# Spreading delta first and du three units ahead, with replanned slots and all low parts as transfers, in a Mamba and MoE layer

## The chip, the cores and the metric

One core of one Trainium2 chip. The metric is the device time of one execution in microseconds (us); the lower, the better. TensorE is called PE here, VectorE DVE, ScalarE ACT, GpSimd POOL and SyncE SP.

## What is computed

The reference is a layer on 32 x 256 tokens of width 128: `x + attn(layernorm(x)) + ffn(layernorm(x))`. `attn` is a Mamba block (inner width 256, 4 heads of 64 channels, 16 states) and `ffn` a mixture of 8 experts with top-1 routing and a capacity of 1024 tokens each.

```python
xz = hidden_states @ in_proj_w.T                    # x, z
x = silu(conv4(x) + conv_b)
dt_r, Bm, Cm = split(x_proj(x))
delta = softplus(dt_proj(dt_r) + dt_proj_b)
def step(s, inp):                                   # over the 256 steps of a sequence
    d_t, u_t, B_t, C_t = inp
    dA = jnp.exp(d_t[..., None] * A)
    s = s * dA + (d_t * u_t)[..., None] * B_t[:, :, None, :]
    y_t = jnp.einsum('bhdn,bhn->bhd', s, C_t)
y = (y + x * Dskip) * silu(z);  out = y @ out_proj_w.T
# ffn: expert_in = dispatch(tokens);  relu(expert_in @ W1 + b1) @ W2 + b2;  combine
```

## The kernel before, in words

**Chunks, units, slots.** The 8192 tokens are cut into 16 chunks (`CHUNKS`) of 512 tokens (`CH`), two sequences each. The 256 channels of a chunk are two halves of 128; each half has 16 units (`UNITS`) of 8 channels x 16 states = 128 rows, so a chunk has 32 units. The main loops of PE, ACT, DVE and POOL all run over chunks and over 32 slots `w` of a chunk (`SLOTS`), `t = 32 * chunk + w`. Each engine has its own in-order queue; semaphores tie them together. A slot number is a place in an engine's program, not a time: the engines are some slots apart.

**One unit.** `delta` and `delta * x` (du) of a half come as high and low parts, stacked by SP in `dsp` (fp32r). PE spreads du to the 128 rows of the unit (`spread_du`, L1228, into one of two banks `du_ps`) and delta likewise (`spread_delta`, L1235, into one of three banks `decay`). ACT turns the latter into `exp(A * delta)` in place (L847). DVE multiplies du by B (`spread_u`, L1006) and runs the scan over time (L1070) into one of eight buffers `s_sb`. POOL multiplies the states by C (L632; in some units, `HELP`, DVE does it, L1057), and PE sums four units at a time into y (`sum_quad`, L1250).

DVE's order is: u product of unit w+1, scan of unit w. In each slot PE first spreads for the unit two slots ahead (`AHEAD = 2`), du before delta, then sums a quad in every fourth slot (`SUM`), then issues the parts of tiles that the tables put there. The waits that matter (L1222 to L1237): du(w) waits until u(w-2) has been read, and delta(w) until the scan of unit w-3 is done.

**The tables.** What lies beside the scan is put into slots by hand-written tables, not by a planner at run time. `STAGE_A` gives, for the next chunk, the tiles x (four parts, L1149), z (L1152), bc and v (L1160) and D (delta, four parts, L1169 and L1171) of both halves, each with its PE slots and the ACT slot that reads it. `FFN_AT` does so for the 16 half-experts (transposes L1192 and L1203, L1195, L1198) in chunks 2 to 14, in a pattern that repeats every three chunks, and `OUT_PROJ` for the output projection (L1180). `SOFTPLUS` and `BY_DVE` give the slots of the softplus steps on ACT and of the four steps on `dd`: `scale` (du = delta * x), `zero`, `high` (ACT, `split_high`, L759) and `low`. `silus` (L710 to L714) is a table load, two silus and a table load on ACT, twice a chunk.

**The low part.** `low = dd - high`. For half (0, 0) and for chunks 3 to 15 POOL issues an accumulating transfer into `dd` (`split_low`, L578). For halves (0,1) to (2,1), the five with `parts_by_dve`, DVE computes it (L1024) and also makes `scale` (L1013) and `zero` (L1018). SP's `stack` (L466) waits for the low part (`low_made`) and issues the four transfers of the half into `dsp` (L472); its queue also spreads B and C (`spread_bc`, L484) and loads the experts.

**Scatters.** In chunks 0 to 2 POOL also issues the 64 indirect transfers that put the tokens into the experts' rows (L638), by `SCATTERED`: seven in eight slots up to slot 63, then one in each up to 71. In chunks 14 and 15 it adds the experts' rows to the output (L613).

The tables that the change touches stand in the diff below.

## Time and profile before

| | us |
|---|---|
| median of 3 runs (lowest, highest) | 1075.68 (1074.43, 1077.33) |
| the profiled execution, its time | 1074.44 |
| its span | 1072.6 |
| first scan starts at | 61.55 |
| mean granted clock of PE | 0.953 |

A row of the timeline gives the start, the duration, the engine, the line and the operation, and in brackets the idle time of the engine before it with what released it; rows of one line that follow each other are merged (x2 and so on). A row of the view of windows is the stretch, its length, the busy time (and count) of PE, PE's weight loads, DVE, ACT and POOL, PE's granted clock, the share of the DMA engines and GB/s. A fp32 matmul of 512 columns is two passes, so two instructions in the counts. The records of neighbouring DVE instructions overlap by some tenths, so distances between starts tell more than durations.

### The profile page before, as it was taken

How to read it: one execution, taken by the hardware profiler on the slowest of the kernel's cores; microseconds unless marked ns; L12 is line 12 of the kernel's file. 1: busy time of each engine (PE TensorE's matmuls, PEld its weight loads, DVE VectorE, ACT ScalarE, POOL GpSimd, SP SyncE). 2: the span in 40 equal slices, each digit the busy share in tenths (PEclk: the TensorE clock that was granted, in tenths of full speed). 3: DMA queues.
4: the chain of work that ended last, by engine and by line, in shares of the span. 5: the costliest groups of instructions: out<-in, count | busy, mean ns of one | idle time of the engine just before them, and what ended most of it. 6: DMA issues, size and time to landing. Idle time of an engine off the chain costs nothing.

```text
span 1072.6 us, 11933 instructions
## 1 busy us (share of the span) xinstructions
PE 963.9 (90%) x3505; PEld 437.5 (41%) x3505; DVE 1007.6 (94%) x1367; ACT 747.3 (70%) x1198; POOL 861.2 (80%) x789
## 2 busy tenths in 40 slices
...
GB/s 268 189 211 97 73 104 95 76 109 123 108 98 116 106 93 82 125 94 97 144 101 91 77 136 87 78 140 106 101 77 143 75 92 90 94 99 117 136 231 37
DMA packets 75324, 121.15 MB, mean 113 GB/s; under 512 B 9294, under 2 KB 38908, under 8 KB 75260
## 3 DMA queue, kind: packets, MB, share of 16 engines
...
## 4 chain that ended last, share of the span: by engine, by line
PE 41%; DVE 24%; ACT 18%; issue 14%; DMA 2%; POOL 1%; SPq 0%; DVEq 0%; ACTq 0%; POOLq 0%
DVE u_sb L1006 10%; DVE s_sb L1070 8%; PE bank L1149 6%; PE bank L1235 6%; PE bank L1198 5%; PE bank L1250 5%; PE bank L1169 5%; PE bank L1228 5%; ACT bank L847 4%; PE bank L1195 3%; PE bank L1160 3%; ACT L714 2%; ACT L710 2%; PE bank L1152 2%; PE bank L1180 1%
## 5 line engine op out<-in xcount | busy, mean ns | idle before, releaser
L632 POOL TENSOR_TENSOR s_sb<-s_sb,c_of 128x512 f32<-128x512 f32 x492 | 643.2, 1343 | 139.5 <-DVE s_sb L1070 134.4
L1070 DVE TENSOR_TENSOR_SCAN s_sb<-bank,u_sb 128x512 f32<-128x512 f32 x512 | 619.6, 1210 | 14.7 <-ACT bank L847 14.4
L847 ACT ACTIVATE bank<-bank,a_neg 128x510 f32<-128x510 f32 x512 | 332.3, 663 | 203.4 <-PE bank L1235 201.7
L1006 DVE TENSOR_TENSOR u_sb<-bank,b_of 128x512 f32<-128x512 f32 x512 | 341.7, 668 | 22.4 <-PE bank L1228 21.4
L1228 PE MATMUL bank<-dsp,sel_d 128*128 128x512 f32 x512 | 327.7, 640 | 16.3 <-DVE u_sb L1006 13.1
L1235 PE MATMUL bank<-dsp,sel_d 128*128 128x512 f32 x512 | 229.7, 449 | 52.9 <-DVE s_sb L1070 49.9
L1228 PEld LDWEIGHTS bank<-dsp,sel_d 128*128 128x128 f32 x512 | 100.5, 196 | 194.9 <-DVE u_sb L1006 109.2
L1235 PEld LDWEIGHTS bank<-dsp,sel_d 128*128 128x128 f32 x512 | 100.9, 197 | 179.9 <-DVE s_sb L1070 134.1
L1250 PE MATMUL bank<-s_sb,con 128*32 128x512 f32 x1024 | 146.3, 645 | 8.1 <-DVE s_sb L1057 5.4
L1149 PE MATMUL bank<-xnT,wx 128*128 128x512 f32 x256 | 133.9, 608 | 0.0
L638 POOL DMA_INDIRECT expert_in<-xn,put_at x64 | 69.7, 1089 | 11.6 <-issue 11.5
L601 POOL DMA_INDIRECT moe<-xn x64 | 64.9, 1013 | 13.2 <-issue 10.1
L1195 PE MATMUL bank<-xn 128*128 128x512 f32 x128 | 66.4, 611 | 4.7 <-ACT xn L763 4.7
L1198 PE MATMUL bank<-xn 128*128 128x512 f32 x128 | 63.3, 602 | 0.0
L1149 PEld LDWEIGHTS bank<-xnT,wx 128*128 128x128 f32 x256 | 47.8, 193 | 27.7 <-issue 20.0
L769 ACT ACTIVATE xn<-bank,b1c 128x512 f32<-128x512 f32 x64 | 43.7, 701 | 18.8 <-PE bank L1195 18.8
L710 ACT ACT_TABLE_LOAD x32 | 41.1, 1283 | 15.4 <-PE bank L1152 15.1
L1169 PE MATMUL bank<-sp_e,con 128*128 128x512 f32 x64 | 36.6, 655 | 6.7 <-ACT xn L769 6.0
L1180 PEld LDWEIGHTS bank<-wzo,g_sb 128*128 128x128 f32 x256 | 34.5, 204 | 17.8 <-issue 15.7
L714 ACT ACT_TABLE_LOAD x32 | 41.1, 1283 | 0.6
L1250 PEld LDWEIGHTS bank<-s_sb,con 128*32 128x32 f32 x1024 | 20.7, 111 | 50.7 <-issue 30.2
L568 POOL TENSOR_TENSOR dd<-dd,xs 128x512 f32<-128x512 f32 x27 | 34.5, 1278 | 7.3 <-ACT dd L753 7.3
...
## 6 DMA issues: line engine op xcount, KB each, us to landing
b_of<-bc SPq DMA_DIRECT2D x64, 256.0 KB, 5.4
c_of<-bc SPq DMA_DIRECT2D x64, 256.0 KB, 6.1
dsp<-neg_hi SPq DMA_DIRECT2D x64, 256.0 KB, 4.1
dsp<-dd SPq DMA_DIRECT2D x64, 256.0 KB, 4.7
...
```

The costliest lines, as they stand in the source:

```text
L632: pool.tensor_tensor(s_now, s_now, c_of[:, hf, hh, :], ALU.mult).then_inc(S["p_ready"], 1)
L638: pool.indirect_dma_start(ein[:, :], bass.IndirectOffsetOnAxis(ap=put_at[:, i:i + 1], axis=0), xn_rows[:, i, :], None).then_inc(S["scatter ...
L847: act.activation(d, d, ACT.Exp, scale=a_neg[:, k:k + 1]).then_inc(S["decay_ready"], 1)
L1006: dve.tensor_tensor(u_sb[:, w % U_RING, :], du_ps[w % 2][:, :], b_of[:, hf, head_of(w), :], ALU.mult).then_inc(S["u_ready"], 1)
L1070: dve.tensor_tensor_scan(s_sb[:, w % S_RING, :], decay_of(w)[:, :], u_sb[:, w % U_RING, :], 0.0, ALU.mult, ALU.add).then_inc(S["scan_done" ...
L1149: mm = pe.matmul(t[:, :], wx[:, hf, part, :], xnT[:, seqs, part:part + SEQ], start=(part == 0), stop=(part == TAPS - 1))
L1169: pe.matmul(t[:, :], ident, (sp_e, sp_r, sp_a)[part], start=(part == 0), stop=False)
L1195: mm = pe.matmul(t[:, :], w1_sb[:, b, x.k * P:(x.k + 1) * P], xeT, start=True, stop=True)
L1198: mm = pe.matmul(t[:, :], w2_sb[:, b, part, :], hT[:, part, :], start=(part == 0), stop=(part == FT - 1))
L1228: pe.matmul(du_ps[w % 2][:, :], sel_d[:, group_of(w), :, :].rearrange("k n d -> k (n d)"), dsp[:, hf, head_of(w), 1, :], start=True, stop= ...
L1235: pe.matmul(decay_of(w)[:, :], sel_d[:, group_of(w), :, :].rearrange("k n d -> k (n d)"), dsp[:, w // UNITS, head_of(w), 0, :], start=True ...
L1250: mm = pe.matmul(y_ps[q * 32:(q + 1) * 32, :], con[:, K_SUM + 32 * r:K_SUM + 32 * (r + 1)], s_sb[:, (QUADS * k + q) % S_RING, :], start=(r ...
```

## The change

PE's slot now begins with delta two units ahead (`DELTA_AHEAD`) and then du three units ahead (`DU_AHEAD`). The waits inside `spread_du` and `spread_delta` stay as they were, and so do the numbers of banks and buffers. The DVE form of `split_low` and its semaphore go; POOL makes all low parts. `scale` and `zero` of the five early halves stay on DVE. The tables are new, with a form of `STAGE_A` of its own for chunks 1 and 2 (`EARLY_A`, nearly the old one).

```diff
-SCATTERED = [min(7 * min(t, 64) // 8 + max(t - 64, 0), TILES) for t in range(3 * SLOTS + 1)]
-HELP = {0: 1, 1: 1}
-SUM = QUADS + 2
-AHEAD = 2
+SCATTERS = (7, 8, 6, 8, 6, 7, 8, 7, 7, 0)
+HELP = {0: (0, 4, 8, 12, 16, 19, 24, 28), 1: (0, 4, 8, 12, 16, 20, 24, 28), CHUNKS - 1: (28, 29, 30, 31)}
+SUM = 6
+DELTA_AHEAD, DU_AHEAD = 2, 3

 STAGE_A = (
+    ("x0", 1, (1, 2, 4, 5), "act", 7), ("z0", 0, (4,), "act", 6.5), ("bc0", 1, (7,), "bc", 9),
+    ("v0", 1, (9,), "act", 11), ("x1", 1, (11, 12, 12, 14), "act", 16), ("z1", 0, (13,), "act", 15.5),
+    ("D0", 0, (15, 15, 16, 16), "act", 18), ("bc1", 1, (20,), "bc", 22), ("v1", 1, (21,), "act", 24),
+    ("D1", 0, (29, 29, 31, 31), "act", 33))
+EARLY_A = (
     ("x0", 1, (0, 1, 3, 4), "act", 6), ("z0", 0, (4,), "act", 5.5), ("bc0", 1, (7,), "bc", 9),
     ("v0", 1, (9,), "act", 11), ("x1", 1, (11, 12, 13, 14), "act", 16), ("z1", 0, (13,), "act", 15.5),
     ("D0", 0, (16, 16, 17, 17), "act", 19), ("bc1", 1, (21,), "bc", 23), ("v1", 1, (23,), "act", 25),
     ("D1", 0, (29, 29, 31, 31), "act", 33))
-OUT_PROJ = (1, (18, 19), "dve", 20)
+OUT_PROJ = (1, (15, 17), "dve", 19)

 FFN_AT = (
-    (2, (0, 19), (0, 21), (0, 23), (1, 25), (0, 25), (1, 27, 27, 28, 28), (0, 34)),
-    (3, (0, 7), (0, 9), (0, 11), (0, 19), (0, 21), (0, 23, 24, 24, 25), (1, 27)),
-    (3, (1, 25), (0, 27), (1, 30), (0, 34), (0, 39), (0, 51, 52, 52, 54), (0, 56)),
-    (4, (1, 25), (1, 27), (0, 27), (1, 30), (0, 34), (0, 39, 40, 40, 41), (0, 43)),
+    (2, (1, 19), (0, 22), (1, 23), (1, 25), (0, 25), (1, 27, 27, 28, 28), (0, 35)),
+    (3, (0, 7), (0, 8), (0, 11), (0, 19), (0, 21), (0, 23, 24, 24, 25), (0, 26)),
+    (3, (1, 23), (0, 27), (1, 31), (0, 32), (0, 39), (0, 50, 51, 52, 53), (0, 57)),
+    (4, (1, 25), (1, 26), (0, 27), (1, 30), (0, 32), (0, 38, 39, 39, 40), (0, 43)),
...

-SOFTPLUS = ({"act": (11, 12, 13, 14), "scale": (17,), "zero": (18,), "high": (22,), "low": (20,)},
-            {"act": (25, 26, 27, 28), "scale": (31,), "zero": (32,), "high": (36,), "low": (34,)})
-BY_DVE = ({"act": (11, 12, 13, 14), "scale": (18,), "zero": (18,), "high": (22,), "low": (21,)},
-          {"act": (25, 26, 27, 28), "scale": (32,), "zero": (32,), "high": (36,), "low": (35,)})
+SOFTPLUS = ({"act": (11, 12, 13, 14), "scale": (17,), "zero": (18,), "high": (22,), "low": (19,)},
+            {"act": (22, 25, 26, 28), "scale": (31,), "zero": (32,), "high": (36,), "low": (34,)})
+BY_DVE = ({"act": (11, 12, 13, 14), "scale": (17,), "zero": (18,), "high": (22,), "low": (19,)},
+          {"act": (25, 26, 27, 28), "scale": (32,), "zero": (32,), "high": (36,), "low": (36,)})
 FIRST_HALF_1 = {"act": (-1, 0, 0, 1), "scale": (4,), "zero": (4,), "high": (7,), "low": (6,)}

             def stack(ch, hf):
-                sp.wait_ge(*low_made(ch, hf))
+                sp.wait_ge(S["lo_by_dma"], 16 * per_chunk(ch, 2, hf + 1))

                     for of, hf_, _ in softplus_now(t, "low"):      # POOL
-                        if not parts_by_dve(of, hf_):
-                            split_low(of, hf_)
+                        split_low(of, hf_)

-            def split_low(ch, hf):                                 # DVE
-                dve.wait_ge(S["hi_ready"], per_chunk(ch, 2, hf + 1))
-                dve.tensor_tensor(dd, dd, neg_hi.bitcast(F32), ALU.add).then_inc(S["lo_by_dve"], 1)

-            for w in range(AHEAD):
-                spread(0, w)
+            for w in range(DELTA_AHEAD):
+                spread_du(0, w)
+                spread_delta(0, w)
+            for w in range(DELTA_AHEAD, DU_AHEAD):
+                spread_du(0, w)
             for ch in range(CHUNKS):
                 for w in range(SLOTS):
-                    if w + AHEAD < SLOTS:
-                        spread(ch, w + AHEAD)
-                    elif ch + 1 < CHUNKS:
-                        spread(ch + 1, w + AHEAD - SLOTS)
+                    for spread, ahead in ((spread_delta, DELTA_AHEAD), (spread_du, DU_AHEAD)):
+                        if w + ahead < SLOTS:
+                            spread(ch, w + ahead)
+                        elif ch + 1 < CHUNKS:
+                            spread(ch + 1, w + ahead - SLOTS)
```

The other twelve rows of `FFN_AT` follow the same pattern, with differences of a slot at most.

## Rows read from the trace of the kernel before

**Rows 1.** The page, busy time and share of each engine
```profile
PE 963.9 (90%) x3505; PEld 437.5 (41%) x3505; DVE 1007.6 (94%) x1367; ACT 747.3 (70%) x1198; POOL 861.2 (80%) x789
```

**Rows 2.** Windows: chunks 0, 1, 2, then 3 to 14 together, then 5
```profile
61.55:131.94 70.39, 60.93 (x167) 24.67 (x167) 67.23 (x82) 41.70 (x64) 58.79 (x49) 0.79 0.54 136
131.94:202.66 70.72, 59.58 (x188) 23.80 (x187) 68.98 (x85) 41.81 (x63) 62.25 (x54) 0.88 0.38 86
202.66:266.65 63.99, 57.95 (x207) 25.12 (x206) 62.35 (x73) 44.66 (x68) 54.25 (x46) 0.97 0.51 118
...
266.65:999.40 732.75, 690.10 (x2598) 319.03 (x2597) 701.40 (x829) 559.33 (x898) 609.52 (x525) 1.00 0.49 102
...
388.65:449.83 61.18, 58.84 (x221) 27.17 (x220) 58.49 (x71) 46.38 (x74) 49.48 (x43) 1.00 0.51 108
```

**Rows 3.** Timeline, DVE, in chunk 5: start us, us, engine, line
```profile
411.12 1.21 DVE L1070 TENSOR_TENSOR_SCAN s_sb<-bank,u_sb 128x512 f32<-128x512 f32 x1
...
412.83 1.21 DVE L1070 TENSOR_TENSOR_SCAN s_sb<-bank,u_sb 128x512 f32<-128x512 f32 x1
...
418.13 0.69 DVE L1006 TENSOR_TENSOR u_sb<-bank,b_of 128x512 f32<-128x512 f32 x1 [0.44 <-PE bank L1228]
...
421.50 1.22 DVE L1070 TENSOR_TENSOR_SCAN s_sb<-bank,u_sb 128x512 f32<-128x512 f32 x1 [0.97 <-ACT bank L847]
```

**Rows 4.** Groups of DVE by line, whole span
```profile
L984 DVE SCALAR_TENSOR_TENSOR bank<-xs,b1c,bank 128x512 f32<-128x512 f32 x32 | 23.3, 728 | 2.1 <-PE bank L1250 2.1
```

**Rows 5.** Waits of DVE, chunks 3 to 14: us, times, longest us
```profile
DVE u_sb L1006 <- PE bank L1228: 17.1, 32, 1.1
DVE s_sb L1070 <- ACT bank L847: 13.5, 26, 1.0
```

**Rows 6.** Timeline, PE, in chunk 5
```profile
411.84 0.39 PE L1235 MATMUL bank<-dsp,sel_d 128*128 128x512 f32 x1
412.07 1.02 PE L1149 MATMUL bank<-xnT,wx 128*128 128x512 f32 x2
...
413.15 0.40 PE L1235 MATMUL bank<-dsp,sel_d 128*128 128x512 f32 x1
...
415.75 1.07 PE L1250 MATMUL bank<-s_sb,con 128*32 128x512 f32 x8
416.74 1.13 PE L1149 MATMUL bank<-xnT,wx 128*128 128x512 f32 x2
```

**Rows 7.** Timeline, ACT, in chunk 5
```profile
417.03 1.28 ACT L710 ACT_TABLE_LOAD   x1
...
420.81 1.81 ACT L847 ACTIVATE bank<-bank,a_neg 128x510 f32<-128x510 f32 x3
```

**Rows 8.** Waits of PE's weight loads, chunks 3 to 14
```profile
PEld bank L1235 <- DVE s_sb L1070: 79.9, 143, 0.9
```

**Rows 9.** Waits of DVE, chunk 15
```profile
DVE u_sb L1006 <- PE bank L1228: 2.4, 3, 1.1
```

**Rows 10.** Instructions on the tile dd: min/median/max ns
```profile
L1024 DVE TENSOR_TENSOR dd<-dd,neg_hi x5: 1341/1841/3011, 77.4 to 210.7; 128x1024 f32<-128x1024 f32 x5
```

**Rows 11.** Timeline: a low part by DVE and one by transfer, and SP's stacking
```profile
77.37 1.61 DVE L1024 TENSOR_TENSOR dd<-dd,neg_hi 128x1024 f32<-128x1024 f32 x1 [1.35 <-ACT neg_hi L759]
...
79.00 0.50 SPq L472 DMA_DIRECT2D dsp<-neg_hi  x1
...
246.43 0.97 POOL L578 DMA_DIRECT2D dd<-neg_hi  x1 [0.40 <-ACT neg_hi L759]
...
251.07 0.50 SPq L472 DMA_DIRECT2D dsp<-neg_hi  x1
```

**Rows 12.** Groups of POOL by line, chunks 0 and 1
```profile
L632 POOL TENSOR_TENSOR s_sb<-s_sb,c_of 128x512 f32<-128x512 f32 x47 | 62.3, 1326 | 29.2 <-DVE s_sb L1070 28.2
L638 POOL DMA_INDIRECT expert_in<-xn,put_at x55 | 59.7, 1085 | 10.2 <-issue 10.0
```

**Rows 13.** The page: a DMA issue of SP, KB each, median us to landing
```profile
dsp<-dd SPq DMA_DIRECT2D x64, 256.0 KB, 4.7
```

More of the change, by code:

```diff
@@ L110 @@
 GATE = (4, 5)
-MOE_ADD_FROM, MOE_ADD_STEP = 14 * 32 + 24, 2
+MOE_ADD_FROM, MOE_ADD_STEP = 472, 2
 MOE_ADD_ORDER = (0, 1, 2, 3, 4, 5, 14, 6, 7, 8, 9, 10, 11, 12, 13, 15)
@@ L254, in stage_a_tiles @@
             return [Tile(name[:-1], of, int(name[-1]), 0, bank_, tuple(first + w for w in slots), by, first + read)
-                    for name, bank_, slots, by, read in STAGE_A]
+                    for name, bank_, slots, by, read in (EARLY_A if of <= DVE_PARTS_TO else STAGE_A)]
         def start_tiles():
@@ L319, in parts_by_dve @@
             return of <= DVE_PARTS_TO and (of, hf) != (0, 0)
-        def low_made(ch, hf):
-            halves = [(c, h) for c in range(ch + 1) for h in range(HALVES) if (c, h) <= (ch, hf)]
-            mine = parts_by_dve(ch, hf)
-            n = sum(parts_by_dve(*x) == mine for x in halves)
-            return (S["lo_by_dve"], n) if mine else (S["lo_by_dma"], 16 * n)
         events = {}
@@ L376, in group_of, with scatters @@
             return w % 2 * QUADS + w % UNITS // QUADS
+        def scatters(t):
+            k, done = t // 8, sum(SCATTERS[:t // 8])
+            n = SCATTERS[k] if k < len(SCATTERS) else 0
+            return range(done + n * (t % 8) // 8, done + n * (t % 8 + 1) // 8)
         def by_dve(ch, w):
-            return w % QUADS < HELP.get(ch, 0) or (ch == CHUNKS - 1 and w >= SLOTS - QUADS)
+            return w in HELP.get(ch, ())
         def products(ch, units):
-            dve = sum(n * SLOTS // QUADS for c, n in HELP.items() if c < ch) + sum(by_dve(ch, w) for w in range(units))
+            dve = sum(len(units) for c, units in HELP.items() if c < ch) + sum(by_dve(ch, w) for w in range(units))
             return dve, ch * SLOTS + units - dve
@@ L636, in _ @@
                         pool.wait_ge(S["routed"], 1)
-                    for i in range(*SCATTERED[t:t + 2]) if t + 1 < len(SCATTERED) else ():
+                    for i in scatters(t):
                         pool.indirect_dma_start(ein[:, :], bass.IndirectOffsetOnAxis(ap=put_at[:, i:i + 1], axis=0),
@@ L1079, in _ @@
                             gate_half(ch, 0, step)
-                    for what, make in (("scale", scale_x), ("zero", zero_first), ("low", split_low)):
+                    for what, make in (("scale", scale_x), ("zero", zero_first)):
                         for of, hf_, _ in softplus_now(t, what):
```

5 lines of the change are left out of this document (1 added, 4 removed), and 24 rows, old and new, of the table FFN_AT.

## The prediction

> **What bounds the kernel now.** I read the page first. VectorE (DVE) is busy 94% of the span, TensorE (PE) 90%, GpSimd (POOL) 80%, ScalarE (ACT) 70% [rows 1]. No share settles it, so the second view is the stretches between the first scans of chunks [rows 2]. Three regimes show. Chunks 0 and 1 take 70.4 and 70.7 us, chunk 2 takes 64.0, and the twelve chunks 3 to 14 take 732.75 us, 61.06 each. In all of them DVE is busy 95% or more.
>
> The third view is one chunk's DVE rows [rows 3]. A unit is one u product and one scan, and undisturbed scans start 1.71 us apart (411.12 to 412.83). 32 units make 54.7 us. The gates and the addition of the out rows are five more instructions, such as L984 with a mean of 0.73 [rows 4], each of which moves the next start by about 0.6, so 3.1 us. DVE's floor is thus about 57.9 us a chunk, against 61.06. The missing 3.2 us are waits of two kinds [rows 5]: in the twelve chunks DVE waits 17.1 us for the spread of du and 13.5 us for decays from ACT (the rest is in waits too small for that view). They are short, at four to seven places of a chunk. Rows 3 shows two, 0.44 us before a u product and 0.97 us before a scan.
>
> Where they come from is seen on PE and ACT. PE's queue is in order. A slot with one fp32 tile part takes 1.31 us (the spreads of delta at 411.84 and 413.15), of which one spread is 0.23 (to 412.07) and two are 0.47, so a part costs 0.84; a quad of sums costs 0.99 (415.75 to 416.74) [rows 6]. Slot 14 of chunk 5 holds a sum and a tile part; the next du stands behind both, and u waits 0.44. On ACT the two silus and their two table loads hold the queue from 417.03 to 420.81, and the exponential behind them makes the scan wait 0.97 [rows 7].
>
> **The change, part by part.**
> (a) *du three units ahead.* No instruction is added. In slot w PE now issues delta(w+2), then du(w+3), then sums and tiles. Compared in order, nothing changes but this: du(w+2) is passed ahead of the sums and tiles of slot w-1. delta(w+2) has the same work ahead of it as before. There are still two du banks, so du(w+3) must wait until u(w+1) is read, which DVE does 0.6 to 0.7 us after the scan that releases delta(w+2). A PE that comes late doesn't notice. A PE that had been waiting for the scan now waits some 0.46 us more (0.7 less the 0.24 of the spread), with the slot's sums, tiles and later deltas queued behind, and ACT behind those. The weight loads of delta wait for a scan 143 times in the twelve chunks [rows 8], so this is frequent. PE can pay: by the counts in the code and the prices above, a chunk is 64 spreads (15.0), 8 quads of sums (8.0), about 66 passes of fp32 tiles at 0.42 (27.7) and 3 us of small ones, 54 of 61 us. What du gains: the work that may stand ahead of it before u waits grows by about 0.8 us; the waits for du are at most 1.1 us. I count 13.6 of the 17.1 us as gained. The rest (a wait of 0.4 to 0.5 at slot 16 in eight of twelve chunks) is followed directly by a wait for the exponential of slot 17, which would only grow. Bounds: 0 and 17.1.
> (b) *New slots.* Nothing is added; D0 is one slot earlier, the expert's output parts one slot earlier, x1's third part beside the second, x0's parts and silu one slot later. In every third chunk (5, 8, 11, 14) ACT is behind all the way to slot 17 and the scan there waits 0.97; earlier expert parts relieve that, 4 x 1.0 = 4 us. The silu of x0 stays as tight as it was. Bounds: all 13.5 us gained, or as much lost again.
> (c) *The price of the new wait.* Some of the added 0.46 reaches ACT at the silus. I take 3 us over the twelve chunks, between 0 and the amount of the third rival.
> Chunks 3 to 14: -13.6 - 4 + 3 = -14.6 us. Chunk 15, where tiles are few but DVE waits 2.4 us for du [rows 9]: -2.
> (d) *Low parts as transfers.* Five instructions leave DVE (halves (0,1), (1,0), (1,1), (2,0), (2,1)), 1.34 to 3.01 us each, median 1.84 [rows 10]; with the one wait before them (1.35) DVE loses about 11.9 us, all on its path. In place of each, POOL issues a transfer (0.97 us, as at 246.43), whose result lets SP stack 4.6 us after the start of the issue (251.07) [rows 11]; other pairs of the 27 take up to 7, one 9. By DVE it was 1.63 us from the start (77.37 to 79.00).
> The Trainium skill (DMA: Bandwidth & Descriptors, Anatomy of one DMA — SWDGE (gpsimd) path) fits a GpSimd-issued transfer at 2.0 us plus its bytes over 436 GB/s, so an estimate of 3.2 us for these 512 KB; by that the first stack would come 1.4 us sooner and the sum would be about 1 us lower. The trace has 4.6, longer than the page.
> What gives way next is POOL. In chunks 0 and 1 it has 24 products at 1.28 us and 28 scatters at 0.99 plus 0.18 of issue, 63.5 us, and its rows there show means of 1.33 and 1.09 [rows 12]; with two lows and their waits for the high part that is 66.5 to 67.5. DVE without the lows needs 54.7 + 8 helped products (4.7) + gates 3.1 + two scalings 2 = 64.5, and with small waits 66. Both chunks come out at about 67.5 instead of 70.5. Chunk 2 has one low fewer, few scatters and is left at 61.5.
> The earliest low, (0,1), is the critical one. Now it is on DVE at 77.37 and SP stacks from 79.00. As a transfer it starts at 77.4 to 79.1 (POOL has a product and a scatter in that slot), stacks from about 83, and with four issues in 3.4 us and 4.7 us of landing [rows 13] is there at 90 to 91. PE asks for it at slot 13, about 87 in the new pace, and DVE needs the first u of the half 3.4 us later, so 0 to 2 us are lost; I take 1. Sum for chunks 0 to 2: -3 - 3.2 - 2.5 + 0.3 (of the late low, what isn't already in the 67.5) = -8.4. Bounds: 0 (POOL and the late lows give it all back) and -14.
> (e) *HELP, SUM, scatters.* HELP has the same eight units, but 19 for 20 in chunk 0; SUM is 6 both times; 64 scatters end at slot 71 in both. 0.
> Total: -14.6 - 2 - 8.4 = -25.0. The profiled execution took 1074.4 us (span 1072.6 and 1.8 around it), so 1049.4; the median of the runs is 1.2 above it, and I give **1050**.
>
> **The rivals.**
> *1. The waits move.* u no longer waits and scans wait for exponentials instead, since ACT's silu blocks stay and DVE reaches them earlier. For: the silu block [rows 7], and the pairs at slots 16 and 17. Against: at slots 29 to 31, 0 and 1, where most of the wait for du is, the exponential is ready in time. Steady gain 4, early 7: 1063. Chance 0.16.
> *2. Nearly all waits go.* The new slots take ACT's waits too: 26 of 30.6 in chunks 3 to 14, 2 in chunk 15, 11 early: 1035. For: PE and ACT have the time (54 and 46 of 61 us). Against: even with PE on time a silu block leaves about 0.3 us: from the scan that releases the exponential before it to the scan that needs the one behind it are three units and a u (5.7), and in between lie the spread (0.45), two exponentials (1.2) and the block (3.8). Chance 0.14.
> *3. Slower: PE blocked at du(w+3).* At the five places of a chunk where DVE waits today, delta (and the tile that a silu needs) comes later by the full 0.7 us: 5 x 12 x 0.7 = +42, less 17.1 for du and 10.4 for the rest: +14.5, 1089. It breaks even at 0.46 us a place. For: 143 waits of delta for the scan. Against: a waiting PE is an early one, and the places are where it is late. Chance 0.08.
> *4. POOL and late lows.* (d) gives nothing, (a) to (c) hold: 1058. For: POOL is 88% busy in chunk 1 [rows 2], and the products wait behind a low that waits for ACT. Chance 0.12.
> *5. The change doesn't do what it says.* Since two banks are all there is, the third unit ahead is never reached in time and only (d) works: 1066. Chance 0.05.
> *6. The clock.* PE's granted clock is 1.00 in chunks 3 to 14 and 0.79 in chunk 0, where PE is less loaded [rows 2], between its levels of 2.4 and 1.2 GHz. Added waits could bring 0.79 to the steady chunks: 54 / 0.79 = 68 us a chunk, +7 x 12 - 10, about 1149. Chance 0.01.
> The Trainium skill (TensorE: Matmul & The Clock Gate, 🔬 Part 1: The HAM clock gate) has the gate close when PE idles; the trace agrees in chunks 0 and 1, and by that page alone this rival would weigh more.
>
> **How the numbers follow.** My forecast has 0.44, with its own range of 1042 to 1057. The range 1034 to 1066 holds it, rival 2 in most of its width, 1, 4 and 5. A measurement of this kernel can tell about 0.3% from no change. Rivals 3 and 6 are slower; a weak form of 1 or 5 could be the same. Faster 0.86, same 0.04, slower 0.10.
>
> **What would show it.** Right: DVE's waits for PE under 5 us in chunks 3 to 14; their stretches near 59.8 us each; chunks 0 and 1 near 67.5, with POOL above 90% busy; no DVE row with the low part; PE waiting on u products for longer in total. Wrong: scans waiting for ACT over 20 us (rival 1) or under 5 (rival 2); chunk 0 still at 70, with PE waiting for the stacked halves (rival 4); du's spread still the releaser of u (rival 5); clock under 1.00 after chunk 2 (rival 6).

## The result and the profile after

The changed kernel takes **1065.57 us** (median of four runs, 1060.80 to 1067.91), the kernel before 1076.39 us beside it; the ratio is 0.9904, with a 95% interval of 0.9888 to 0.992. By this ratio it is 10.3 us faster (10.8 by the medians), where 25 were forecast. The profiled execution is the slowest of the four: 1067.91 us, span 1065.8, 6.8 us under the span before.

Busy shares hardly move: VectorE (DVE) has 9 us less of work, the low parts.

```profile
PE 958.1 (90%) x3505; PEld 434.3 (41%) x3505; DVE 998.7 (94%) x1362; ACT 748.1 (70%) x1198; POOL 860.2 (81%) x794
```

The windows between the first scans of chunks answer to [rows 2]: chunks 0, 1, 2, then 3 to 14, then 5, 6 and 11. The columns are the stretch and its length, busy time of PE, PEld, DVE, ACT and POOL with instruction counts, granted clock, DMA share and GB/s.

```profile
60.78:132.04 71.26, 56.45 (x166) 22.05 (x165) 65.25 (x79) 41.64 (x64) 58.78 (x51) 0.88 0.61 150
132.04:201.31 69.27, 58.11 (x188) 23.47 (x188) 64.94 (x82) 41.19 (x62) 62.64 (x56) 0.88 0.47 103
201.31:263.99 62.68, 56.38 (x207) 25.48 (x206) 59.98 (x72) 44.50 (x68) 54.67 (x47) 0.97 0.56 129
263.99:995.66 731.67, 693.38 (x2597) 318.65 (x2598) 701.50 (x829) 561.18 (x898) 607.76 (x525) 0.99 0.49 102
382.40:446.50 64.10, 60.26 (x223) 27.89 (x222) 59.16 (x70) 47.25 (x75) 52.01 (x45) 0.97 0.49 104
446.50:505.90 59.40, 56.91 (x222) 26.46 (x223) 58.05 (x70) 47.71 (x78) 49.69 (x44) 1.00 0.47 96
749.10:814.80 65.70, 61.40 (x223) 28.34 (x222) 59.18 (x70) 47.26 (x75) 52.14 (x45) 0.95 0.48 102
```

The difference in span is the sum of: start to first scan -0.8, chunk 0 +0.9, chunk 1 -1.5, chunk 2 -1.3, chunks 3 to 14 -1.1, and from the first to the last scan of chunk 15 -3.1 (59.88 to 56.81). The steady chunks, where 14.6 us had been expected, give 1.1 in this execution; in e4, e8, e9 and e10 below, where these chunks have the same order and tables, they give 5.7 to 6.4. They are no longer alike: eight take 59.1 to 60.9 us, against 61.06 before, while 5, 8, 11 and 14 take 64.1, 62.9, 65.7 and 62.1.

DVE's waits in chunks 3 to 14 answer to [rows 5] (us, times, longest), and PE's waits of a new kind stand under them:

```profile
DVE s_sb L1069 <- ACT bank L851: 18.6, 21, 1.5
DVE s_sb L1069 <- PE bank L1245: 4.3, 10, 1.2
DVE u_sb L1010 <- PE bank L1227: 3.4, 7, 0.8
...
PE bank L1227 <- DVE u_sb L1010: 7.6, 19, 0.7
...
PE bank L1159 <- ACT bc L727: 5.4, 3, 2.1
```

The waits for du are gone as foreseen (17.1 to 3.4), but the scans' waits for exponentials rose from 13.5 to 18.6 us, in fewer and longer pieces, and PE now waits for the read of `bc`, which its list of waits didn't hold before. (ACT did wait for the transfer before, 4.6 us in four pieces, but no matmul stood behind it.)

The timeline of chunk 5 shows both. DVE is at unit 17 in the first line; then come ACT, and PE:

```profile
416.18 1.22 DVE L1069 TENSOR_TENSOR_SCAN s_sb<-bank,u_sb 128x512 f32<-128x512 f32 x1 [1.51 <-ACT bank L851]
...
423.10 1.06 ACT L763 ACTIVATE neg_hi<-dd 128x1024 fp32r<-128x1024 f32 x1
425.90 0.59 ACT L727 ACTIVATE bc<-bank 64x512 f32<-64x512 f32 x1 [1.74 <-DMA c_of<-bc]
...
424.44 0.50 PE L1227 MATMUL bank<-dsp,sel_d 128*128 128x512 f32 x1 [0.43 <-DVE u_sb L1010]
426.54 1.23 PE L1159 MATMUL bank<-xs,weff 128*128 128x512 f32 x2 [1.61 <-ACT bc L727]
...
428.56 1.93 PE L1245 MATMUL bank<-s_sb,con 128*32 128x512 f32 x8
```

The read of the tile bc1, moved from slot 23 to 22, stands idle for 1.74 us until the transfer of the half before has left its buffer; PE, which needs the bank for v1, waits 1.61 us behind it. Then a quad of sums takes 1.93 us where it took 1.07 in [rows 6]. That is the clock: the next view cuts chunk 11, whose wait was 2.06 us, into windows of 2 us from 788 on.

```profile
788.00:790.00 2.00, 2.00 (x9) 0.89 (x7) 2.00 (x4) 1.99 (x4) 1.92 (x4) 1.00 0.85 200
790.00:792.00 2.00, 1.13 (x3) 0.37 (x2) 2.00 (x3) 0.79 (x1) 1.56 (x3) 1.00 0.78 117
792.00:794.00 2.00, 0.36 (x1) 0.37 (x2) 2.00 (x4) 1.01 (x2) 2.00 (x3) 0.67 0.82 162
794.00:796.00 2.00, 2.00 (x4) 0.81 (x3) 2.00 (x3) 0.12 (x1) 1.81 (x2) 0.50 0.63 117
796.00:798.00 2.00, 2.00 (x10) 0.20 (x8) 0.86 (x2) 1.82 (x3) 1.27 (x1) 0.50 0.49 104
798.00:800.00 2.00, 2.00 (x7) 0.89 (x4) 1.22 (x1) 0.02 (x1) 0.20 (x1) 0.63 0.99 223
```

PE is busy 1.49 us of the four from 790 on, and the granted clock goes from 1.00 to 0.50, that is from 2.4 to 1.2 GHz, for some six us in which PE never rests. DVE runs dry meanwhile (0.86 of 2 us busy).

In chunk 0 the low part of half (0,1) is the case of [rows 11]; POOL's issue, SP's first stacking, and the first users of the half:

```profile
78.30 0.99 POOL L583 DMA_DIRECT2D dd<-neg_hi  x1
...
83.25 0.50 SPq L477 DMA_DIRECT2D dsp<-neg_hi  x1
...
90.16 0.80 PE L1227 MATMUL bank<-dsp,sel_d 128*128 128x512 f32 x1 [3.30 <-DMA dsp<-dd]
...
171.90 1.22 DVE L1017 TENSOR_TENSOR dd<-dd,xs 128x512 f32<-128x512 f32 x1 [2.79 <-ACT dd L757]
```

The half is there at 90.1, inside the forecast 90 to 91, but costs 3.3 us of PE. The last line is in chunk 1: DVE's scaling, planned for slot 17 now, meets the tile D0 that ACT reads at 19, and DVE stands for 2.79 us.

### The profile page after: what moved, and what is told of

It is laid out like the page before. It is cut to its first block, busy times and chain, and to the rows that moved or that the text cites. A ratio compares the mean times of both kernels' runs of the same rounds, so it can differ in the third digit from the quotient of the medians.

```text
span 1065.8 us, 11933 instructions
## 1 busy us (share of the span) xinstructions
PE 958.1 (90%) x3505; PEld 434.3 (41%) x3505; DVE 998.7 (94%) x1362; ACT 748.1 (70%) x1198; POOL 860.2 (81%) x794
## 4 chain that ended last, share of the span: by engine, by line
PE 39%; DVE 15%; issue 13%; ACT 12%; DMA 10%; POOL 8%; SPq 3%; DVEq 0%; POOLq 0%; ACTq 0%
DVE u_sb L1010 8%; PE bank L1245 5%; POOL s_sb L637 5%; PE bank L1148 5%; PE bank L1227 5%; PE bank L1168 4%; PE bank L1234 4%; DMA dd<-neg_hi 4%; PE bank L1197 4%; DVE s_sb L1069 4%; DMA dsp<-dd 4%; PE bank L1194 3%; PE bank L1159 3%; ACT bank L851 2%; POOL expert_in L643 2%
## 5 line engine op out<-in xcount | busy, mean ns | idle before, releaser
L1234 PE MATMUL bank<-dsp,sel_d 128*128 128x512 f32 x512 | 316.4, 618 | 22.7 <-DVE s_sb L1069 22.4
L1227 PE MATMUL bank<-dsp,sel_d 128*128 128x512 f32 x512 | 223.7, 437 | 40.4 <-DVE u_sb L1010 31.1
L1234 PEld LDWEIGHTS bank<-dsp,sel_d 128*128 128x128 f32 x512 | 99.0, 193 | 215.4 <-DVE s_sb L1069 139.5
L1227 PEld LDWEIGHTS bank<-dsp,sel_d 128*128 128x128 f32 x512 | 100.0, 195 | 139.5 <-DVE u_sb L1010 86.4
L1194 PE MATMUL bank<-xn 128*128 128x512 f32 x128 | 69.0, 624 | 11.4 <-ACT xn L773 3.6
L643 POOL DMA_INDIRECT expert_in<-xn,put_at x64 | 66.2, 1034 | 12.0 <-issue 11.6
L1197 PE MATMUL bank<-xn 128*128 128x512 f32 x128 | 63.5, 599 | 0.1
L583 POOL DMA_DIRECT2D dd<-neg_hi x32 | 30.7, 959 | 23.7 <-ACT neg_hi L763 23.5
L1159 PE MATMUL bank<-xs,weff 128*128 128x512 f32 x64 | 36.3, 651 | 6.4 <-ACT bc L727 5.6
```

What stands on the lines that cost most here:

```text
L643: pool.indirect_dma_start(ein[:, :], bass.IndirectOffsetOnAxis(ap=put_at[:, i:i + 1], axis=0), xn_rows[:, i, :], None).then_inc(S["scatter ...
L1159: pe.matmul(t[0:4 * NS, :] if x.kind == "bc" else t[:, :], w[:, hf, :], xs_of(x.of, hf), start=True, stop=True).then_inc(S["misc_pe"], 1)
L1194: mm = pe.matmul(t[:, :], w1_sb[:, b, x.k * P:(x.k + 1) * P], xeT, start=True, stop=True)
L1197: mm = pe.matmul(t[:, :], w2_sb[:, b, part, :], hT[:, part, :], start=(part == 0), stop=(part == FT - 1))
L1227: pe.matmul(du_ps[w % 2][:, :], sel_d[:, group_of(w), :, :].rearrange("k n d -> k (n d)"), dsp[:, hf, head_of(w), 1, :], start=True, stop= ...
L1234: pe.matmul(decay_of(w)[:, :], sel_d[:, group_of(w), :, :].rearrange("k n d -> k (n d)"), dsp[:, w // UNITS, head_of(w), 0, :], start=True ...
```

## The experiments

All chunk lengths in one table, from one profiled execution each, in us from first scan to first scan; "long" are chunks 5, 8, 11 and 14, "short" the other eight of 3 to 14. Times are medians, ratios are to the kernel before on the same chip. Single executions differ in the first chunks: up to the end of chunk 0 the changed kernel, e6, e8, e11 and e13 are one program, and their chunk 0 takes 70.1 to 72.1 us, with granted clocks of 0.80 to 0.88.

| kernel | chunks 0, 1, 2 | short | long | 3 to 14 | time, ratio [95%] |
|---|---|---|---|---|---|
| before | 70.4, 70.7, 64.0 | 61.0 to 61.1 | 61.1 to 61.2 | 732.8 | 1076.39 |
| changed | 71.3, 69.3, 62.7 | 59.1 to 60.9 | 62.1 to 65.7 | 731.7 | 1065.57, 0.9904 [0.9888, 0.992] |
| e1 order only | 69.3, 70.0, 67.1 | 60.8 to 62.5 | 62.6 to 62.9 | 744.0 | 1083.97, 1.0083 [1.006, 1.0106] |
| e2 lows only | 66.7, 69.7, 67.9 | 61.0 to 61.1 | 61.0 to 61.2 | 732.8 | 1071.83, 0.9969 [0.9956, 0.9981] |
| e3 tables only | 71.6, 70.4, 65.3 | 60.4 to 62.3 | 62.3 to 64.6 | 747.2 | 1088.32, 1.0125 [1.0106, 1.0145] |
| e4 order and tables | 70.4, 72.5, 64.4 | 59.0 to 60.9 | 61.5 to 63.0 | 726.5 | 1069.41, 0.995 [0.9934, 0.9967] |
| e5 order, x0 later | 71.2, 70.3, 65.1 | 60.1 to 60.3 | 61.2 to 61.8 | 728.0 | 1068.69, 0.9942 [0.9924, 0.9959] |
| e6 old slots 19 to 26 | 70.1, 69.2, 62.9 | 59.7 to 60.9 | 61.4 to 62.1 | 729.2 | 1066.29, 0.9926 [0.9906, 0.9946] |
| e7 scale at 18 | 68.9, 67.9, 66.2 | 59.1 to 60.9 | 62.3 to 65.9 | 729.9 | 1064.58, 0.9894 [0.9867, 0.9921] |
| e8 more help | 72.1, 69.2, 64.0 | 59.1 to 60.9 | 61.4 to 62.9 | 726.4 | 1064.22, 0.9913 [0.9881, 0.9945] |
| e9 one low on DVE | 69.5, 69.2, 62.7 | 59.2 to 60.9 | 61.4 to 63.4 | 727.0 | 1066.03, 0.9933 [0.9911, 0.9956] |
| e10 e7 and e8 | 69.1, 69.4, 64.0 | 59.1 to 60.9 | 61.5 to 63.0 | 726.7 | 1063.02, 0.9909 [0.9884, 0.9934] |
| e11 mixed tables | 70.1, 69.2, 62.7 | 59.3 to 60.3 | 60.9 to 61.9 | 723.0 | 1058.74, 0.9859 [0.984, 0.9878] |
| e12 e9, e10, e11 | 67.9, 69.4, 64.0 | 59.2 to 60.2 | 61.0 to 61.9 | 722.2 | 1061.97, 0.9894 [0.987, 0.9918] |
| e13 second silus later | 71.2, 69.3, 66.6 | 61.8 to 63.7 | 63.4 to 65.0 | 761.2 | 1101.36, 1.023 [1.0205, 1.0256] |

**e1: the order alone**, on the kernel before.

```diff
-AHEAD = 2
+DELTA_AHEAD, DU_AHEAD = 2, 3
...
-                        spread(ch, w + AHEAD)
+                    for spread, ahead in ((spread_delta, DELTA_AHEAD), (spread_du, DU_AHEAD)):
+                        if w + ahead < SLOTS:
+                            spread(ch, w + ahead)
```

> The kernel before with only the new order of the spreads (delta two units ahead, then du three), every table and the low parts as before. Theory A (the new order gives, single slots of the new tables take back): waits of DVE for du fall from 17.1 to under 6 us in chunks 3 to 14, every third chunk (5, 8, 11, 14) is not longer than 61.2 us, and the time is 8 to 16 us below the kernel before, about 1064. Theory B (PE waiting at du(w+3) is what lengthens chunks 5, 8, 11 and 14): those chunks are at 62 to 65 us here too and the time is within 4 us of the kernel before.

It is slower by 0.8%. Neither theory gives that: du's waits are gone as in A, chunks 5, 8, 11 and 14 are long as in B, but five of the other eight are longer too. Chunks 3 to 14 of its trace, DVE's waits, then PE's:

```profile
DVE s_sb L1070 <- ACT bank L847: 39.1, 34, 1.9
...
PE bank L1235 <- DVE s_sb L1070: 16.4, 36, 0.7
PE bank L1228 <- DVE u_sb L1006: 15.4, 24, 1.3
```

The wait for du has left the list, and the waits for exponentials went from 13.5 to 39.1 us. PE's own waits for DVE's u and scans come to 31.8 us in 60 pieces, against 26.7 for scans alone before: 5.1 more. The timeline of a boundary, chunk 4's unit 7, shows what holds:

```profile
341.45 1.28 ACT L710 ACT_TABLE_LOAD   x1 [1.31 <-PE bank L1152]
...
345.24 1.24 ACT L847 ACTIVATE bank<-bank,a_neg 128x510 f32<-128x510 f32 x2
...
345.93 1.22 DVE L1070 TENSOR_TENSOR_SCAN s_sb<-bank,u_sb 128x512 f32<-128x512 f32 x1 [1.83 <-ACT bank L847]
```

From scan 30 to scan 7 it took 18.64 us before (322.86 to 341.50) and takes 18.83 now (327.10 to 345.93). In both, PE works almost without pause from the first part of D1 (slot 29) to the tile of z0 (slot 4), 13.70 and 13.78 us; then come two table loads and two silus (3.8 us) and the exponential of unit 7. The u products were waiting inside a stretch whose end the silus set. Earlier du lets DVE come earlier to the same place.

That explains why nothing was gained there, not the loss. The loss lies further on. This table gives the time between scans of these units, summed over the twelve chunks, worked out from the starts of the scans (30 is that of the chunk before):

| kernel | 30 to 7 | 7 to 13 | 13 to 17 | 17 to 30 |
|---|---|---|---|---|
| before | 220.3 | 123.4 | 96.1 | 292.8 |
| e1 | 221.5 | 124.2 | 102.1 | 295.8 |
| e5 | 201.9 | 126.2 | 104.1 | 295.8 |
| e4 | 204.0 | 127.0 | 99.5 | 295.9 |
| changed | 204.5 | 127.0 | 100.0 | 300.0 |
| e11 | 201.7 | 127.0 | 100.2 | 294.3 |

Over half of e1's loss, 6.0 us, is between scans 13 and 17, ahead of the second silu block: the scans' waits at unit 17 go from 7.6 to 15.6 us. PE's timeline in chunk 6 shows why, around slot 9. First the kernel before, then e1:

```profile
466.72 0.50 PE L1235 MATMUL bank<-dsp,sel_d 128*128 128x512 f32 x1 [0.63 <-DVE s_sb L1070]
467.06 1.02 PE L1195 MATMUL bank<-xn 128*128 128x512 f32 x2
```

```profile
472.50 0.50 PE L1235 MATMUL bank<-dsp,sel_d 128*128 128x512 f32 x1 [0.63 <-DVE s_sb L1070]
473.08 0.19 PEld L1228 LDWEIGHTS bank<-dsp,sel_d 128*128 128x128 f32 x1 [0.40 <-DVE u_sb L1006]
473.42 1.02 PE L1195 MATMUL bank<-xn 128*128 128x512 f32 x2
```

In both, PE has waited for the same scan. In e1 a du stands between the delta and the tiles, and its weight load waits for a u product, so the tiles begin 0.92 us after the delta, not 0.34. From there to unit 17 PE's timeline has no pause in either kernel, so the tiles stay 0.58 us later, ACT's second silu block starts 0.36 us later after scan 9 and scan 17 comes 0.36 us later. This is the new wait of (c), where it costs. It was followed in this one chunk; ten of the twelve lose 0.3 to 0.5 us between scans 13 and 17.

**e2: the low parts alone**, on the kernel before.

```diff
-                        if not parts_by_dve(of, hf_):
-                            split_low(of, hf_)
+                        split_low(of, hf_)
...
-"high": (22,), "low": (21,)}
+"high": (22,), "low": (19,)}
```

> The kernel before with only the five early low parts as transfers of POOL, at the slots of the change (19 and 36). Theory A (the saving on DVE is mostly lost to the later stacking in chunk 0): chunks 0 and 1 at 68 to 70.5 us, PE waiting 1 to 3 us for the stacked half (0,1), and the time 4 to 7 us below the kernel before. Rival (the lows leave DVE at no price): 11 to 12 us below. Other rival (POOL and late stacking take it all): no difference.

Faster by 3.3 us by the ratio, 3.1 by the medians, under the 4 to 7 of theory A. In the profile chunk 0 gives 3.7 us and chunk 1 gives 1.0, but chunk 2 takes 3.9 more, and PE waits 1.8 us for the stacked half. This execution, the slowest of six, doesn't show where the times gain: its first scan comes 1.5 us later than before, and chunk 15, where nothing is changed, is 1.5 us shorter. PE's waits in chunk 2:

```profile
PE bank L1249 <- POOL s_sb L632: 5.5, 2, 3.8
PE bank L1234 <- DVE s_sb L1069: 2.4, 6, 0.6
```

POOL's products are late there. That POOL, 87 and 90% busy in chunks 0 and 1, leaves a backlog which chunk 2 pays is argued here; e10 bears it out.

**e3: the tables alone**, on the kernel before: `STAGE_A`, `EARLY_A`, `OUT_PROJ`, `FFN_AT`, `SOFTPLUS` and the rest between them as in the change, with the low parts and the scaling on DVE as before.

```diff
-                    for name, bank_, slots, by, read in STAGE_A]
+                    for name, bank_, slots, by, read in (EARLY_A if of <= DVE_PARTS_TO else STAGE_A)]
```

> The kernel before with only the new tables for inputs, softplus, experts and out rows (low parts on DVE in their old slots, old order of the spreads). Theory A (bc1 read at slot 22 makes ACT wait for the transfer that still reads the tile bc in every third chunk): chunks 5, 8, 11 and 14 at 63 to 66 us, the others at or below 61, the time 0 to 8 us above the kernel before. Theory B (the tables are good and the order is at fault): all chunks at or below 61 and the time 4 to 10 us below.

Slower by 1.25%, 13.4 us, where theory A had 0 to 8: three of the four long chunks are as it says, but six of the other eight are longer than 61.2 us too. In chunks 3 to 14 no scan waits for ACT any more, and every wait is for du:

```profile
DVE u_sb L1012 <- PE bank L1234: 44.5, 59, 2.2
```

**e4: order and tables**, the edits of e1 and e3 together.

> The change without its low parts: new order and new tables, with the five early low parts on DVE in their old slots. Both theories: chunks 3 to 14 as in the changed kernel (731 us together). Theory A (low parts as transfers gain little, because the stacking of half (0,1) comes late): within 4 us of the changed kernel, 1064 to 1069. Rival (they gain their full 11.9 us on DVE): 1076 to 1078.

Alone, the parts cost 11.2 (e1) and 14.4 us (e3) over chunks 3 to 14; together they give 6.2. So the tables are no ornament of the order: with x0's silu a slot later the exponential that e1 waits for comes before the block, and with du ahead the slots that e3 packs densely no longer hold u up. The long chunks 5 and 11 take 62.8 us here, at a granted clock of 1.00, with PE waiting 1.8 us at the same place as in the changed kernel; there they take 64.1 and 65.7. The rest of the change (the lows as transfers, with the scaling a slot earlier and small shifts of scatters and helped units) is 1069.4 to 1065.6, or 4.9 us by the ratios.

**e5: one table entry.** e1, with x0 and z0 one slot later in the tiles of chunk 3 and later.

```diff
-    ("x0", 1, (0, 1, 3, 4), "act", 6), ("z0", 0, (4,), "act", 5.5), ("bc0", 1, (7,), "bc", 9),
+    ("x0", 1, (1, 2, 4, 5), "act", 7), ("z0", 0, (4,), "act", 6.5), ("bc0", 1, (7,), "bc", 9),
```

> The kernel of the first experiment (new order alone) with one edit more: from chunk 3 on the tile x0 and the silus of half 0 stand one slot later, as in the change. Theory P (PE works through slots 29 to 4 without a pause, and that run and the silu block behind it set when the decay of unit 7 is there; the new order only moves DVE's wait from du to that decay): the 1.0 to 1.9 us wait of the scan at slot 7 falls to 0 to 0.8 at slot 8, chunks 3 to 14 fall from 744 to 724 to 732 us, the time to 1064 to 1072. Theory B (PE's waits for u products, which stay, are what costs): chunks 3 to 14 stay over 738 us, the time over 1078.

Chunks 3 to 14 fall from 744.0 to 728.0 us: of what the tables do for the order (17.5 us) this one line does 16. The waits at unit 7, 18.5 us in e1, are gone; those at unit 17 stay (16.5). The same stretch of ACT, with the exponential of unit 7 now ahead of the block at 338.64, and scan 7 without a wait:

```profile
338.64 0.66 ACT L852 ACTIVATE bank<-bank,a_neg 128x510 f32<-128x510 f32 x1 [0.68 <-PE bank L1240]
339.31 1.28 ACT L715 ACT_TABLE_LOAD   x1
...
343.10 1.23 ACT L852 ACTIVATE bank<-bank,a_neg 128x510 f32<-128x510 f32 x2
...
343.84 1.22 DVE L1075 TENSOR_TENSOR_SCAN s_sb<-bank,u_sb 128x512 f32<-128x512 f32 x1 [0.22 <-issue]
```

Its long chunks take 61.2 to 61.8 us, not 62 to 65: what makes them long came with the other slots.

**e6: bc1, v1, softplus of half 1 and the experts' slots 19 to 26 as before**, on the changed kernel.

```diff
-("bc1", 1, (20,), "bc", 22), ("v1", 1, (21,), "act", 24)
+("bc1", 1, (21,), "bc", 23), ("v1", 1, (23,), "act", 25)
...
-            {"act": (22, 25, 26, 28), "scale": (31,)
+            {"act": (25, 26, 27, 28), "scale": (31,)
```

> The changed kernel with the tiles bc1 and v1, the softplus steps of half 1 and the expert tiles of slots 19 to 26 in their old slots. Theory C (in chunks 5, 8, 11 and 14 ACT reads bc1 so early that it waits 1.7 to 2.2 us for the spread of C, PE waits for ACT, and its clock falls): those four chunks go from 62.1 to 65.7 to 61 to 62.5 us, granted clock 1.00 in all of 3 to 13, the time 4 to 8 us below the changed kernel, about 1059, with less spread. Rival (the wait is only passed on, or the old slots cost the other eight chunks as much): within 2 us of the changed kernel.

The long chunks are mended (61.4 to 62.1, with no clock under 1.00 in 5, 8 and 11), but the short ones grow by 0.65 on average, so the sum is 729.2 and the time that of the rival. As a group the new slots are right for eight chunks and wrong for four. Four things are undone at once here, so that bc1's read is the one that matters is argued from PE's waits behind it, not shown.

**e7: DVE's scaling of half 0 at slot 18**, in chunks 0 and 1 of the changed kernel.

```diff
-BY_DVE = ({"act": (11, 12, 13, 14), "scale": (17,),
+BY_DVE = ({"act": (11, 12, 13, 14), "scale": (18,),
```

> The changed kernel with the early scaling of du by DVE at slot 18 again, not 17. Theory L (in chunk 1 POOL is the limit, so DVE's wait of 2.95 us for D0 costs nothing): the wait is gone and chunk 1 stays within 0.8 us of 69.3. Rival (DVE is the limit there): chunk 1 at 66 to 67 us and the time 2 to 4 us below the changed kernel.

DVE's waits for D0 in chunk 1 shrink from 4.0 to 1.9 us and the chunk gets 1.4 us shorter, but chunk 2 gets 3.6 longer. PE's and DVE's longest waits there are POOL's backlog again:

```profile
PE bank L1245 <- POOL s_sb L637: 3.3, 1, 3.3
...
DVE s_sb L1069 <- PE bank L1245: 2.6, 2, 2.4
```

**e8: six products more on DVE** (two in chunk 1, four in the first seven slots of chunk 2).

```diff
-HELP = {..., 1: (0, 4, 8, 12, 16, 20, 24, 28), ...}
+HELP = {..., 1: (0, 4, 8, 12, 14, 16, 20, 22, 24, 28), 2: (0, 2, 4, 6), ...}
```

> The changed kernel with DVE making two more products in chunk 1 (slots 14 and 22) and four in chunk 2 (0, 2, 4, 6). Theory L (POOL limits chunks 1 and the start of 2): each takes 1.28 us from POOL and adds 0.6 to DVE, chunk 1 falls from 69.3 to about 67, chunk 2 stays within 1 us, the time 1 to 4 us below the changed kernel. Rival (DVE is the limit): chunks 1 and 2 longer by 1.2 and 2.4 us, the time 3 us above.

Chunk 1 stays at 69.2 us, since DVE's waits for D0 are still there (3.8 us), and chunk 2 gets 1.3 longer. Its time, 1064.2, is within the spread of the changed kernel's runs; so is that of e7.

**e9: one low part, half (0,1), on DVE.**

```diff
+        def low_by_dve(of, hf):
+            return (of, hf) == (0, 1)
```

> The changed kernel with one low part, that of half 1 of chunk 0, made on VectorE again; the others stay transfers. Theory H (the handoff costs there): in chunk 0 of the changed kernel GpSimd issues this transfer at 78.3 us and SyncE stacks from 83.25 on, after which the product of unit 16 waits 3.3 us for it. With the low part on VectorE the stack starts about 2.5 us earlier, the waits of unit 16 fall under 1 us, and chunk 0 goes from 71.3 to about 68.5 us (1.3 to 1.8 us of VectorE's time come back); the time goes to about 1063 us. Rival R (the time is VectorE's and GpSimd's load, not the handoff): chunk 0 stays over 70.4 us, what it had with all low parts on VectorE, and the time stays at 1065 to 1067 us. Chunks 3 to 14 should be those of the changed kernel under both: 59 to 60 us, 61 in chunk 9, 62 to 66 in 5, 8, 11 and 14.

SP stacks at 78.28 where it was 83.25, no wait for the stacked half is left, and chunk 0 takes 69.5 us, 1.8 less; I had expected 68.5. The time, 1066.0, doesn't show it: four runs span 1061.1 to 1068.8, more than what is sought. So that the wait goes is shown, what it is worth isn't. 69.5 is only 0.6 under the range of one and the same program (70.1 to 72.1), and e7 and e10, in which PE still waits 3.2 and 3.4 us for the half, have 68.9 and 69.1. Against e10, e12 takes 1.2 us less in chunk 0.

**e10: e7 and e8 together.**

> The changed kernel with both edits of the two runs before together: VectorE's scale of half 0 a slot later (18) in chunks 0 and 1, and six products more on VectorE (two in chunk 1, four in the first seven slots of chunk 2). Theory G (GpSimd's backlog takes what VectorE gains): with the products taken from GpSimd the waits of chunk 2 that the later scale brought (3.3 us of PE for a product, 2.5 us of the scan at slot 12) go, chunk 1 keeps 67.5 to 68.5 us and chunk 2 goes from 66.2 to 64 us; first three 202 to 203.5, and the time is 1063 to 1065 us: the two engines together are near their limit here, so no more than 1 us comes from this. Rival R: chunk 2 stays at 66 us, so its waits have another cause than the products on GpSimd; 1065 to 1067 us.

Chunk 2 falls from 66.2 to 64.0 us, and the wait for POOL's products goes, as theory G has it. But DVE, with two products more in chunk 1, then takes 69.4 there, not 68. The first three chunks take 202.6 us, 0.6 less than in the changed kernel. DVE is busy 67.35 of chunk 1's 69.4 us and POOL 60.3: what one gives the other takes.

**e11: mixed tables.** The four long chunks keep the old slots of bc1, v1, half 1's softplus and the experts; chunk 9's expert rows take the slots of chunk 6's.

```diff
+STAGE_A_LONG = STAGE_A[:7] + (("bc1", 1, (21,), "bc", 23), ("v1", 1, (23,), "act", 25)) + STAGE_A[9:]
+LONG = (6, 9, 12, 15)
...
+                if of in LONG and hf == 1:
+                    table = dict(table, act=(25, 26, 27, 28))
...
-    (5, (0, 19), (0, 22), (1, 23), (1, 25), (0, 25), (1, 27, 27, 28, 28), (0, 35)),
+    (5, (0, 19), (0, 21), (0, 23), (1, 25), (0, 25), (1, 27, 27, 28, 28), (0, 35)),
```

> The changed kernel, in which only the tiles made in chunks 5, 8, 11 and 14 (and the expert tiles that start in 5, 8 and 11 from slot 19 on) have the old slots of bc1, v1 and softplus of half 1, and the two expert rows that begin in chunk 9 have the slots of those of chunk 6. Theory L (in these four chunks alone bc1 is read too soon behind its copy, and ScalarE has two experts' work there): they fall to 61.5 to 62 us as with the old slots everywhere, the other eight keep 59.1 to 60.0 (chunk 9 59.3), and the twelve sum to about 722 us where they were 731.7; granted clock 0.99 or more in all of them; the time is about 1056 us, 0.981 of the kernel before. Rival M (slots of a chunk act on the next, so mixed tables do no better than either): the eight grow by 0.5 to 1 us each as they did with the old slots everywhere, the sum stays at 727 to 730 us, and the time at 1063 to 1066 us.

Windows of chunks 3 to 14, 5 and 6:

```profile
263.97:986.94 722.97, 688.74 (x2598) 316.40 (x2599) 698.81 (x828) 561.47 (x898) 606.85 (x525) 1.00 0.50 103
383.78:445.64 61.86, 59.44 (x223) 27.51 (x222) 58.40 (x70) 47.34 (x75) 51.34 (x45) 1.00 0.51 108
445.64:504.97 59.33, 56.78 (x222) 26.27 (x222) 57.99 (x70) 47.75 (x78) 50.17 (x44) 1.00 0.47 96
```

Theory L holds: 723.0 us where 722 were expected. 1058.74 us is the best of all versions, 0.9859 of the kernel before; its interval (0.984 to 0.9878) lies wholly under the change's. Its four runs lie within 2.5 us, those of the changed kernel within 7.1 (e12's, with the same mixed tables, within 6.6). What remains of waits is the second silu block and the backlog of the long chunks: scans wait 17.8 us for ACT, 19 times.

**e12: e9, e10 and e11 together.**

> The edits of the three runs of this batch together: low part of chunk 0's half 1 on VectorE, scale at 18, six products more on VectorE, and the mixed tables. If they add (theories H, G and L): chunk 0 68.5, chunk 1 68, chunk 2 64, chunks 3 to 14 722 us, and the time is 1052 to 1055 us. Rival: what is gained in chunk 0 is lost again in chunks 1 and 2, the first three stay at 203 us, and the time is that of the mixed tables alone, 1056 us, or, if those do nothing, 1064.

The profiled execution, the fastest of four, takes 1057.68 us with 201.3 us for the first three chunks and 722.2 for the next twelve; the median is 1061.97, over e11's. The edits of the first chunks show no gain in the times, and whether they lose is not settled: the runs span 6.6 us.

**e13: the second silus later.** e11, with ACT's reads of x1 and z1 at slots 17 and 16.5 for 16 and 15.5; the matmuls stay.

```diff
-    ("v0", 1, (9,), "act", 11), ("x1", 1, (11, 12, 12, 14), "act", 16), ("z1", 0, (13,), "act", 15.5),
+    ("v0", 1, (9,), "act", 11), ("x1", 1, (11, 12, 12, 14), "act", 17), ("z1", 0, (13,), "act", 16.5),
```

> The version with mixed tables (e11, 1058.7 us), in which from chunk 2 on ScalarE's silus of x1 and z1 also stand a slot later (reads 17 and 16.5 for 16 and 15.5); the matmuls stay where they are. Theory P (the wait at unit 17 is the block of two table loads and two silus ahead of its exponential): the exponential of unit 17 is made before the block and that of unit 18 behind it, a slot nearer to where ScalarE has slack; as with x0 and z0 (744 to 728 us for twelve chunks) the wait at 17 goes and less comes at 18: chunks 3 to 14 lose 0.5 to 1 us each, 723 becomes 711 to 717 us, and the time 1048 to 1053 us. Rival Q (PE waits for bank 1 and bank 0, that of the out rows and of D0, until the later silus have read them, and deltas behind them come late): the wait only moves to unit 18 at the same length or grows, PE's idle time grows by 1 us or more in each chunk, chunks 3 to 14 take 723 to 740 us, and the time is 1059 to 1075 us.

Slower by 2.3%, worse than rival Q's 1075. PE's waits in chunks 3 to 14, then chunk 6's timeline:

```profile
PE bank L1173 <- ACT zs L719: 29.1, 12, 2.4
```

```profile
489.11 1.28 ACT L719 ACT_TABLE_LOAD   x1
...
491.05 1.29 PE L1173 MATMUL bank<-sp_e,con 128*128 128x512 f32 x2 [2.42 <-ACT zs L719]
492.14 1.91 PE L1173 MATMUL bank<-sp_r,con 128*128 128x512 f32 x2
...
496.10 0.69 DVE L1015 TENSOR_TENSOR u_sb<-bank,b_of 128x512 f32<-128x512 f32 x1 [5.25 <-PE bank L1232]
```

The wait at unit 17 has gone in chunks 3 to 14, as theory P said, so it is the second silu block. But D0's matmuls need the bank that z1's silu frees; PE stands 2.4 us in each of twelve chunks, again falls to a lower clock (`sp_r` parts take 1.91 us for two where 1.02 is usual), and u of unit 18 waits 3.0 to 5.3 us. At the first block the next tiles of both banks start at slots 6 to 8, about with the later reads (7 and 6.5); here D0 starts at 15 and the out rows too, ahead of the reads at 16.5 and 17.

## Why the prediction was wrong

The sign held, and the range (1034 to 1066) by 0.4 us, which is luck; the size, 25 us, was two and a half times the 10.3 measured, and my own forecast's range (1042 to 1057) was missed.

**(a) du ahead, 13.6 of 17.1 us.** This is the step that failed. That du's waits would end was right (17.1 to none in e1). That their time would be gained was not: e1, which is (a) with its price (c), forecast at -10.6, costs 11.2 us over chunks 3 to 14. I priced each wait by its own length and asked only at unit 16 what would be late next. At slots 29 to 1 I took the exponential as "ready in time" and looked no further than that place; but unit 7, six to ten units on, stood behind PE's queue and the silu block, whose end did not move: scan 30 to scan 7 takes 221.5 us in e1 for 220.3.

**(b) New slots, -4.** Undersized and of the wrong kind. With the order, the tables give 17.5 us (744.0 to 726.5), 16 of them from the one line for x0. I had read that line in the diff and written that its silu "stays as tight as it was": wrong, since the move puts unit 7's exponential ahead of the block. The 4 us for every third chunk went the other way. Those chunks take 61.5 to 63.0 us in e4 where they took 61.1 to 61.2; e6 and e11 show that the new slots from 19 on are at fault, by undoing them together. In the profile of the change the lower clock comes on top.

**(c) Price of the new wait, +3.** Undersized as well. The mechanism is as foreseen, and its size at one place nearly so (0.58 us for 0.46), but it counts in full ahead of unit 17: scans 13 to 17 take 6.0 us more in e1, though the waits for du that stood there are gone. How much of e1's 11.2 us it makes in all wasn't separated. PE's waits for u and scans are a poor measure of it: they grew by 5.1 us in e1, and fell to 14.6 in the changed kernel (7.6 for u, 7.0 for scans). Rival 3's mechanism exists, then, and with the old tables the new order is a loss; at 11.2 us it is far from the net 24.9 (42 less 17.1) that rival 3 puts on the new order.

The sum (a) to (c) was -14.6: measured -6.2 in e4, -6.4 in e8, -5.7 in e9 and -6.1 in e10 for chunks 3 to 14, and -1.1 in the profile of the change, in whose chunks 5 and 11 the mean granted clock was 0.97 and 0.95. In e4 the stretch from scan 30 to scan 7 gives 16.3 us, and the other three take 10.1 back.

**Chunk 15, -2.** Measured -3.1, of which single executions may account for half: e2 has -1.5 there with nothing changed.

**(d) Lows as transfers, -8.4.** Measured -1.9 over chunks 0 to 2 in the profile, -3.1 by e2's medians, -3.8 by the medians of e4 and the change. The handoff was timed well (landed at 90.1), but PE waited 3.3 us for it, not 1; what undoing it is worth isn't clear of the noise of chunk 0 (1.8 us in e9, 1.2 from e10 to e12). Chunk 1 came to 69.3, not 67.5: 2.8 us of it are DVE's wait for D0, since the change moves the scaling to slot 17 while ACT reads D0 at 19. I had counted two scalings at their duration and didn't look at what the earlier slot waits for. e7 shows the rest: with that wait halved POOL falls behind and chunk 2 pays (67.9 and 66.2 for 69.3 and 62.7). POOL as next limit was named, but I let it bound each chunk by itself; its backlog passes from one chunk to the next.

**(e)** was 0. It wasn't tested by itself.

**The rivals.** Rival 1 (the waits move to the exponentials; 1063, chance 0.16) is what happened in the steady chunks, though its sign, scans waiting for ACT over 20 us, is just missed with 18.6 (e1 has 39.1). Rival 4's late half added to it, and its sign is there: chunk 0 at 71.3 us with PE waiting for the stacked half. Of the signs of being right, du's waits under 5 us (3.4) and PE's waits on u products came, but the steady chunks averaged 60.97 us, not 59.8, and chunks 0 and 1 took 71.3 and 69.3, not 67.5. Rival 6 gave chance 0.01 to clock drops in the steady chunks; they came, not for whole chunks but for some 4 to 6 us at a time, behind one PE wait of 1.6 to 2.1 us, and in some executions only.

Open: how e1's 11.2 us divide between the two blocks' causes; what decides whether the clock falls after a pause of PE; and whether the edits of the first three chunks gain anything that times can show.
